# Second attention layer: the front of the next batch made inside the heads, and the heads unrolled

## What is computed

```python
def adaln(x, c, g, w, b):
    scale, shift = jnp.split(bitlinear(c[:, None, :], w, b), 2, axis=-1)
    return rmsnorm(x, g) * (1 + scale) + shift
def bitlinear(x, w, b):                      # 8-bit activations, ternary weights
    return act_quant(x) @ weight_quant(w).T + b
xn = adaln(x, c, g1, w_ada1, b_ada1)
q, k, v = split(bitlinear(xn, w_qkv, b_qkv)) # 16 heads of 32 channels
attn = softmax(q @ k.T * 32 ** -0.5)
x = x + bitlinear(concat(attn @ v), w_proj, b_proj)
```

## Time and profile before

| | us |
|---|---|
| median of 3 runs | 3204.18 (3201.48 to 3204.37) |
| profiled execution, its own time | 3200.36 |
| span of the profiled execution | 3198.6 |
| PE busy | 2873.3 (90%) |
| DVE busy | 2314.5 (72%) |
| POOL busy | 1944.9 (61%) |
| ACT busy | 1783.0 (56%) |

### The profile page before, as it was taken

How to read it: one execution, slowest core, us unless ns; L and a number is a source line. 1 busy time by engine, 2 the same in 40 slices (tenths; PEclk the granted TensorE clock), 3 DMA queues, 4 the chain that set the end, 5 groups by cost and what they waited for, 6 DMA issues and landing times. The chain is left out here.

```text
span 3198.6 us, 71752 instructions
## 1 busy us (share of the span) xinstructions
PE 2873.3 (90%) x21895; PEld 1421.1 (44%) x21943; DVE 2314.5 (72%) x4526; ACT 1783.0 (56%) x3191; POOL 1944.9 (61%) x1627
## 2 busy tenths in 40 slices
PE   7999999998999999999499979997999799937887
PEld 4454444444445444444144434543454345413443
DVE  3677666776577656775777787778777877639997
ACT  2366444664266633664356656665666566636766
POOL 0288615884088912886368857885788578832221
PEclk9999999999999999999799989998999899969999
DMA  5022321232222331221312222222222222250000
GB/s 178 21 54 56 133 73 47 50 116 80 66 51 50 97 109 47 59 52 57 112 41 60 67 73 58 54 70 73 58 50 82 66 53 54 56 216 31 28 28 30
DMA packets 88795, 220.44 MB, mean 69 GB/s; under 512 B 16300, under 2 KB 18452, under 8 KB 87448
## 3 DMA queue, kind: packets, MB, share of 16 engines
q1 hardware_dynamic: 86920, 211.67, 23.5%
q0 software_dynamic: 1680, 6.33, 0.5%
HBM read 84.72 MB, written 31.51 MB: 36 GB/s over the span
## 5 line engine op out<-in xcount | busy, mean ns | idle before, releaser
L433 DVE TENSOR_REDUCE b_mxs<-ps 128x1 f32<-128x512 f32 x1024 | 636.8, 683 | 198.9 <-PE ps L323 197.5
L433 DVE TENSOR_REDUCE a_mxs<-ps 128x1 f32<-128x512 f32 x1024 | 636.0, 683 | 183.3 <-PE ps L323 181.9
L406 ACT ACTIVATE b_p<-ps 128x512 f32<-128x512 f32 x1024 | 532.6, 600 | 218.9 <-PE ps L337 212.3
L406 ACT ACTIVATE a_p<-ps 128x512 f32<-128x512 f32 x1024 | 530.9, 601 | 213.3 <-PE ps L337 208.1
L295 POOL TENSOR_TENSOR b_sum<-b_p 128x512 f32<-128x512 f32 x384 | 502.9, 1314 | 76.1 <-ACT b_p L406 76.1
L295 POOL TENSOR_TENSOR a_sum<-a_p 128x512 f32<-128x512 f32 x384 | 498.3, 1301 | 77.1 <-ACT a_p L406 76.9
L323 PE MATMUL ps<-b_k,b_q 96*128 96x512 f32 x1024 | 447.6, 441 | 16.9 <-DVE b_mxs L433 9.5
L323 PE MATMUL ps<-a_k,a_q 96*128 96x512 f32 x1024 | 439.9, 439 | 4.0 <-DVE a_xv L932 3.4
L337 PE MATMUL ps<-b_q,b_k 98*128 98x512 f32 x1024 | 403.9, 429 | 24.2 <-ACT b_p L406 21.2
L337 PE MATMUL ps<-a_q,a_k 98*128 98x512 f32 x1024 | 399.4, 424 | 14.4 <-ACT a_p L406 14.2
L351 PE MATMUL ps<-b_p,b_vx 128*32 128x512 f32 x2048 | 371.8, 599 | 17.1 <-POOL b_sum L300 11.7
(11 more groups left out here) (213 smaller groups left out, 3919.7 us busy)
## 6 DMA issues: line engine op xcount, KB each, us to landing
a_q<-a_qh SPq DMA_DIRECT2D x128, 128.0 KB, 2.3
a_k<-a_kh SPq DMA_DIRECT2D x128, 128.0 KB, 2.4
b_q<-b_qh SPq DMA_DIRECT2D x128, 128.0 KB, 2.3
b_k<-b_kh SPq DMA_DIRECT2D x128, 128.0 KB, 2.4
a_kl<-in_x SPq DMA_DIRECT2D x4, 2048.0 KB, 8.4
a_q<-a_ql SPq DMA_DIRECT2D x64, 128.0 KB, 2.3
a_k<-a_kl SPq DMA_DIRECT2D x64, 128.0 KB, 2.3
a_kh<-in_x SPq DMA_DIRECT2D x4, 2048.0 KB, 14.6
```

Source lines behind the costliest of these rows:

```text
L406: act.activation(self.key_tile(u, kt), self.st[RING[CHUNKS * (k % NJ) + n]], ACT.Exp, scale=self.scale).then_inc(self.s_exp, 1)
L433: dve.reduce_max(self.mxs[:, c:c + 1], self.mx[RING[CHUNKS * j + c]], axis=AX.X).then_inc(self.s_mxr, 1)
```

## The change

- `loop` gets a flag `flat`: all 17 head indices are written out in `layer1a`. Each engine gets a hook `extra(k, s)`, called at the end of step s of head k.
- SP loads x of the next batch (in two halves) and its modulation at head 5, after the loads of head 8 and once rows 0 and 1 of the staged Q and K have been read out. It loads the first three heads of the next batch before `work`, and the residual x, into the upper half of the exponentials' tile `p` (`xres`), once the last `values_round` is done. The bias of V goes the same way, into a tile of `sum`.
- VectorE norms one tile in each of heads 5 to 12, in steps 2 (scale), 4 (shift) and 6 (maximum). `end_front` follows in head 13, step 2, the clipping to bf16 in head 14, steps 2 to 5, the two copies of R in steps 6 and 7. The waits for x and modulation (`loads`) stand in head 5, step 2, ahead of the first scaling.
- ScalarE rounds one tile a step from head 13, step 4, to head 14, step 3.
- TensorE makes R, X and QK 0 to 7 in heads 14 to 16, by the table `SLOT`, in banks 3 to 5. The units 0 to 7 leave through VectorE in head 15, step 3, to head 16, step 2, each with its low part a step behind.
- The maximum of the attended rows is taken over 384 channels in head 15 and over the last 128 in `work` (`largest`).
- `work` between batches is left with QK 8 to 15, T, Y and V, in this order: QK 8 to 11, T, QK 12 and 13, Y, QK 14 and 15, V. The parts of the first two heads' maxima begin after QK 9. Each of QK 8 to 15 has a buffer of its own. In the `work` ahead of batch 0 the first eight units get their low part from VectorE, right behind the unit.

```diff
@@ -229,6 +229,10 @@
             n = 4 * i + k
             ok = (lambda kk: 0 <= 4 * i + kk < H) if known else (lambda kk: True)
             head(i, k, H * b + n, ok, 5 if known and n == H else STEPS)
+        if flat:
+            for k in range(H + 1):
+                call(0, k, True)
+            return
         call(0, 0, True)
         with eng.Fori(0, NQ - 1) as i:
             for k in range(1, NJ + 1):
...
         tokqT = halves[:, :, 1, :].rearrange("p t (k c) -> p k t c", k=KC)
 
         late = [t[:, :, :].bitcast(FP32).rearrange("p k t -> p (k t)") for t in stage]
-        xn = late[3].rearrange("p (t d) -> p t d", t=TT)
+        xn = [late[3 if t < 4 else 1][:, t % 4 * D:(t % 4 + 1) * D] for t in range(TT)]
         xq = late[2][:, 0:2 * T].bitcast(BF16).rearrange("p (t d) -> p t d", t=TT)
         xq = [xq[:, t, :] for t in range(TT)]
+        mod_r = late[0][:, 0:2 * D].rearrange("p (i d) -> p i d", i=2)
         diag = late[2][:, 2 * T:3 * T].rearrange("p (t c) -> p t c", t=TT)
...
+        xres = att.p[:, 4:8, :].rearrange("p a (h n) -> p (a h) n", h=2)
+
+        def qf(v):
+
+            if v < EARLY:
+                return late[v % 4 // 2][:, 3 * T + v % 2 * HALF:3 * T + (v % 2 + 1) * HALF]
+            return att.p[:, (v - EARLY) // 2, v % 2 * HALF:(v % 2 + 1) * HALF]
 
         UNITS = [(m, c) for q in range(KC) for m in (q, KC + q) for c in range(2)]
-        OWN = 4
+        EARLY = 8
         BANKS = (0, 1, 2, 6)
+        FIRST = [("R", n) for n in range(2)] + [("X", n) for n in range(KC)] + [("QK", n) for n in range(EARLY)]
+        SLOT = {(14, 3): (0,), (14, 4): (1,), (14, 6): (2, 3), (14, 7): (4,), (15, 0): (5,), (16, 0): (12,), (16, 2): (13,)}
+        SLOT |= {(15, s): (s + 4,) for s in range(2, STEPS)}
 
         def parts(v):
...
-            left = {kind: iter(range(n)) for kind, n in kinds.items()}
-            order = [(kind, n) for kind, take in (("X", KC), ("R", 2), ("QK", 10), ("T", KC), ("QK", 2), ("Y", TT),
+            kinds = {"X": range(KC), "R": range(2)} if nxt and not tail else {}
+            kinds |= {"QK": range(EARLY if tail else 0, UN), "V": range(TT)} if nxt else {}
+            kinds |= {"T": range(KC), "Y": range(TT)} if tail else {}
+            left = {kind: iter(n) for kind, n in kinds.items()}
+            order = [(kind, n) for kind, take in (("X", KC), ("R", 2), ("QK", 4 if tail else 10), ("T", KC), ("QK", 2), ("Y", TT),
                                                   ("QK", 2), ("V", TT), ("QK", 2))
                      for n in islice(left.get(kind, ()), take)]
-            at = order.index(("QK", 9)) + 1 if nxt else len(order)
+            at = (1 if tail else order.index(("QK", 9)) + 1) if nxt else len(order)
             return [(kind, n, BANKS[i % len(BANKS)], order[i - len(BANKS)] if i >= len(BANKS) else None,
                      i - at if 0 <= i - at < att.PRELUDE else None) for i, (kind, n) in enumerate(order)]
         MT = 10
...
+                    def late_load():
+                        sp.dma_start(bp, rows(ins["b_proj"], P)).then_inc(s_late, 16)
+
+                    def extra(n):
+                        if n == 5 and not last:
+                            for j in range(NJ):
+                                sp.wait_ge(att.s_load[j], att.LD * (NQ * b + 2))
                             front(b + 1)
-                        sp.dma_start(bp, rows(ins["b_proj"], P)).then_inc(s_late, 16)
-                    att.run_sp(sp, b, late)
-                    sp.wait_ge(att.s_vx, H * (b + 1))
-                    sp.dma_start(xv[:, :, :], x_in[bass.ds(b * T, T), :].rearrange("(t p) d -> p t d", p=P)).then_inc(s_res, 16)
+                    att.run_sp(sp, b, late_load, extra)
+                    if not last:
+                        att.first_loads(sp, b + 1)
+                    sp.wait_ge(att.s_pv, 2 * att.ROUNDS * H * (b + 1) + att.PV_CREDIT)
+                    if not last:
+                        sp.dma_start(bv, rows(ins["b_v"], P)).then_inc(s_bv, 16)
+                    sp.dma_start(xres, x_in[bass.ds(b * T, T), :].rearrange("(t p) d -> p t d", p=P)).then_inc(s_res, 16)
...
                 def attend(b, last):
+                    def extra(n, s):
+                        if last:
+                            return
+                        for e in SLOT.get((n, s), ()):
+                            if e == 0:
+                                pe.wait_ge(att.s_mxr, CHUNKS * H * (b + 1) + att.MX_CREDIT)
+                            if e >= 3:
+                                pe.wait_ge(KINDS[FIRST[e - 3][0]][2], count(*FIRST[e - 3], b + 1, None))
+                            product(*FIRST[e], ps[:, 3 + e % 3, :], b + 1, None)
                     pe.wait_ge(s_val, TT * (b + 1))
                     pe.wait_ge(s_qf, UN * (b + 1))
-                    att.run_pe(pe, b)
+                    att.run_pe(pe, b, extra)
                     pe.wait_ge(att.s_o, 2 * H * (b + 1) + 2)
...
+                    def extra(n, s):
+                        if last:
+                            return
+                        if 13 * STEPS + 4 <= n * STEPS + s < 14 * STEPS + 4:
+                            round_(0, b + 1, n * STEPS + s - 13 * STEPS - 4)
+                        if n == 15 and s < 2:
+                            for k in (2 * s, 2 * s + 1):
+                                transposed("X", k, ps[:, 3 + (2 + k) % 3, :], b + 1, None)
+                        v = (n - 15) * STEPS + s - 4
+                        if 0 <= v < EARLY:
+                            high(v, b + 1, None)
                     act.wait_ge(s_lo, UN * (b + 1))
...
+                def largest(ch, t, part):
+
+                    cols = slice(0, 12 * HD) if part == 0 else slice(12 * HD, D)
+                    ch.mark(dve.tensor_reduce(amx[:, t, part:part + 1], tok[:, t, cols], AX.X, ALU.max, apply_absolute_value=True))
...
+                    def extra(n, s):
+                        if n == 15 and s < 4:
+                            if s == 0:
+                                dve.wait_ge(att.s_o, 2 * (H * b + 12) + 2)
+                            for t in (2 * s, 2 * s + 1):
+                                largest(cht, t, 0)
                         if last:
                             return
-                        if i == 0:
-                            loads(b + 1)
-                        if i > 0 and (i - 1) // 2 < pairs + 2:
-                            ch.wait()
-                        for stage_ in range(3):
-                            pair = i // 2 - stage_
-                            if 0 <= pair < pairs:
-                                norm(ch, b + 1, 2 * pair + i % 2, stage_)
-                        if i == 2 * (pairs + 2):
+                        if 5 <= n < 5 + TT and s in (2, 4, 6):
+                            if n == 5 and s == 2:
+                                loads(b + 1)
+                            if s > 2:
+                                ch.wait()
+                            norm(ch, b + 1, n - 5, s // 2 - 1)
+                        if n == 13 and s == 2:
                             end_front(ch)
-                    att.run_dve(dve, b, spare)
...
                 def work(order, nxt, tail):
                     if tail is not None:
-                        ch = Chain(dve, s_vt, SC * tail, SC)
+                        cht = tails["chain"]
                         dve.wait_ge(att.s_o, 2 * H * (tail + 1) + 2)
-                    for t in range(TT):
-                        if tail is not None:
-                            absmax(ch, 1, tok, t)
-                        if nxt is not None:
-                            eight_bits(0, nxt, t, xn, xq)
-                    if tail is not None:
-                        scales(ch, 1, W_AT["proj"])
-                        ch.close()
...
+                        cht.mark(dve.tensor_reduce(am[:, 1, 0, :], amx[:, :, :], AX.X, ALU.max))
+                        scales(cht, 1, W_AT["proj"])
+                        cht.close()
+                    if nxt is not None and tail is None:
+                        for t in range(TT):
+                            eight_bits(0, nxt, t)
                     if nxt is None:
                         for t in range(TT):
-                            eight_bits(1, tail, t, tok, tokq)
```

323 lines of the change are left out of this document (176 added, 147 removed).

## The result

The changed kernel takes 3223.2 us (median of 4, 3218.3 to 3226.5) where the kernel before takes 3203.8 (median of 4 beside it). The ratio is 1.0061, with a 95% interval from 1.0043 to 1.0078: **19.5 us slower**, and above the range of the prediction. The profiled execution took 3224.1 us, with a span of 3222.1 and a mean clock of 0.963.

A forecast was written before the change was run, and what follows sets the result against it. TensorE was taken to set the pace in the heads, a chain through VectorE, ScalarE and TensorE between batches; three batches -15.3, +5.8 and -4.5 made -14.0, so 3190 us; 8 in 10 from 3163 to 3215.

The forecast's parts named there:

- The stage between batches: From the last division to the first score waiting for an exponential of the next batch: 25.6 us shorter a batch.
- Heads 14 to 16: Transposes, R and eight units added on TensorE, 39.8 us of work, make these heads 5 us longer a batch.
- Rival C: Heads 14 to 16 grow by 12 us instead of 5, engines handing over single units in order: 3211; chance 0.13.
- Head 5, the new wait: VectorE stands some 6.3 us before the loads of x and modulation, TensorE waits: +8 us a batch, between 5 and 10.
- Rival B: The stall in head 5 does not come: 8 us less a batch, 3166; chance 0.12.
- Heads 5 to 12: Norming one tile a head on VectorE costs 0.6 us a head, +5 a batch, between 2 and 10.
- Head 13: Scales and diagonal, 3.7 us within a burst where TensorE can go on for 1.1: +2.5 us, between 1 and 3.5.
- Ahead of batch 0: In the stage there, each of eight units waits for ScalarE's high part before the next leaves: +5.8 us, once.
- Behind batch 3: Scales ready 2.7 us after the last head's end instead of 7.1: -4.5 us, once.
- Unrolling: Writing out the loop of heads costs nothing, as the windows contain the loop's jumps and TensorE has no gap.
- Rival A: In heads 5 to 12 every scaling and shift waits for a whole GpSimd addition, 2 us a head: 3223; chance 0.15.

The follow-up runs named there:

- the probes: Changed kernel, next batch's norm left out, one VectorE probe instruction in each of heads 6 to 12; pitches 15.4, 15.1, 15.4, 14.7, 14.7, 16.2, 15.4 us.
- e_flat: Kernel before with only the 16 heads of the second layer's attention written out on every engine: 3199.1 us beside 3203.8, ratio 0.9987.

## Why the prediction was wrong

Term by term, a batch unless said otherwise:

- *The stage between batches*, -25.6: **right**, -26.4 and -26.7 in the two that were measured to the load of the table.
- *Heads 14 to 16*, +5: **right in size**, +4.7, +3.6 and +7.7, 5.3 in the mean; in part by luck, as the window of batch 0 shows:

```profile
1871.70:1911.70 40.00, 34.20 (x359) 14.42 (x350) 26.59 (x50) 28.24 (x50) 26.57 (x21) 0.99 0.14 30
```

  TensorE is busy for 34.2 us, not for the 39.8 that I had added up, and idle for 5.8 instead of 0.7, so it isn't the limit as I had said. Rival C's sign is there, one wait of 1.96 us for ScalarE's copy in each batch, but not its 12 us: as a size C fell. In batch 2 the granted clock of this stretch is 0.92, and TensorE is busy 3 us longer with the same matmuls.
- *Head 5, the new wait*, +8 and the 0.6 of its norm: **right**, +8.7, and the mechanism too: VectorE idle for 5.80 us, ended by the modulation, TensorE behind it. Rival B fell. It is no price of the work, though: begun five steps later, the same work has no stall.
- *Heads 5 to 12*, +0.6 a head: **wrong, the mis-sized term**. In heads 6 to 12 it is 1.6 us (11.1 for the seven instead of 4.2). I took the scaling at the median beside GpSimd, 0.95 of the earlier trace rows. There the eight scalings last anything from 0.75 to 1.53 us. In these heads the phase repeats: 1.63 us in every one, above even the maximum of the earlier trace rows. The slack of 0.5 that I gave the burst is about right (the probes show 0.3). The shift costs nothing, as said.
- *Head 13*, +2.5, between 1 and 3.5: **wrong**, +7.3 to +7.7. The 3.7 us were read from the earlier trace rows. Between the rows shown there stand, by VectorE's timeline of the kernel before:

```profile
1861.32 1.08 DVE L1285 TENSOR_SCALAR b_am<-b_am,dws 128x8 f32<-128x8 f32 x1
1862.43 1.20 DVE L1287 TENSOR_SCALAR b_am<-b_am 128x8 f32<-128x8 f32 x1
```

  So two of the three small `TENSOR_SCALAR` had waited there already and only the first, 0.17, had not. In head 13 all three do, and the five take 4.9 us, 1.1 more. TensorE goes on for 1.2 us, as I had said, but then needs the third reduction as well, 0.6 us that I left out: that makes its wait of 4.3. The largest price is the half clock after that wait, which I left out too: some 2.5 us, as the five microseconds of the window are spent on what takes 2.5. In head 5 I had put such a price in, here not. These come to 6.8 us; the rest of the 7.3 to 7.7 stays open.
- *Ahead of batch 0*, +5.8 once: **right**, +6.4 for what the change does; the execution that was profiled began 4.8 later on top.
- *Behind batch 3*, -4.5 once: -2.5 by the spans from the last division on (389.5 and 387.0). The scales are ready 2.6 us after it, as laid out, and the first clipping comes 4.5 us earlier than before. Of this the first product of the projection keeps 4.1, and the last addition of the residual 3.2; what takes it wasn't tried.
- *Unrolling*, 0: 4 us less in a launch by the ratio of `e_flat`; in its profile batch 3 is 2.2 us shorter than in the kernel before, and the three others together 1.2 longer.

Put together: 3 x (-26.4 + 4.8 + 8.7 + 11.1 + 7.5) = +17.1, then +6.4 + 4.8 - 2.5 - 2 = +23.8; the two spans differ by 23.5. Most of these terms are read from batch 0, and they agree better in the sum than one by one. Exactly, from one first row-maximum part of a batch to the next, the changed kernel is 12.4 us longer ahead of batch 0, then 7.8, 3.4 and 7.2, then 4.7 shorter in batch 3 and 2.5 behind it. The medians differ by 19.5, 4 less than these two executions. The two mis-sized terms make 3 x (6.9 + 5.0) = 36 us; with them the forecast of 3190 would have been 3226.

Rival A named what happened in the heads: the scaling waits for the addition, and from 1.2 us a head on the gain is gone. It had a chance of 0.15. That its time of 3223 us is the measured one is luck: it had 2 us a head, 11 a batch above the forecast, and 0.5 us a head of that by the shift, which costs next to nothing; the heads gave 6.9 above it, and head 13, for which A had no price of its own, 5.0. I gave 1.63 us the place of an exception because a median stood against it; the argument for it, that in a head each scaling meets a GpSimd that works 88% of the time, was the better one. The Trainium skill's "SBUF — State Buffer", "Who interferes with whom", says that whoever issues first has the shared ports for its whole instruction, that a product of two operands in SBUF and the faster mode of `tensor_scalar` need them, and that a reduction on trn2 doesn't. The traces agree with that rule in the cases shown here: 1.63 and 1.10 us for products and bounds that came second, 0.67 and 0.16 for maxima.
